# A macaron block of routed feed-forward, attention and routed feed-forward on one core: earlier gathers, sums moved from VectorE to GpSimd, and other orders where the program changes part

## The chip, the core and the metric

The kernel runs on one core of a Trainium2 chip. Its engines are TensorE (PE in the profile; its weight loads PEld), VectorE (DVE), ScalarE (ACT), GpSimd (POOL) and SyncE (SP), which issues most of the DMAs; each works through its own program in order and meets the others at semaphores. The metric is the device time of one execution in microseconds (us), the median of several.

## What is computed

```
x = x + 0.5 * ffn(layernorm(x))       # x: 16 sequences x 512 tokens x 128, float32
x = x + attention(layernorm(x))       # 16 heads of 8, keys = queries = values less their mean
x = x + 0.5 * ffn(layernorm(x))       # the same weights again

ffn(x):  probs = softmax(x @ Wg + bg); w, idx = top_k(probs, 2); w = w / sum(w)
         h = relu(x @ W1[e] + b1[e])  # 8 experts, 256 hidden
         y = h @ W2[e] + b2[e]
         out = sum over e of y[e] * weight of e
attention(x): c = x - mean over the tokens;  softmax(c @ c.T) @ x, head by head
```

## The kernel before

A *dense job* is one sequence that runs through all 8 experts and is multiplied by gates that are zero for the six not chosen. A *routed job* sends each token's row to its two experts: rows are scattered to DRAM (`sorted`), tiles of one expert are run through it in a *tile stream* and stored (`tiles`), and the results are gathered back (`found`), multiplied by their gates and added to x. The program has these parts, in time: dense jobs 0 to 6 of the first feed-forward (0 to 201 us); attention of sequences 0 to 4; a stream of 25 tiles for the nine routed jobs 0 to 8; attention of sequences 5 to 13 (from 449 us), with the routed results gathered and added beside it; a stream of 31 tiles for the twelve routed jobs 9 to 20 of the second feed-forward; attention of sequences 14 and 15 (from 839 us); and dense jobs 7 to 10 (from 899 us), the tail, beside which the routed jobs 9 to 20 are gathered and added. Attention is four head groups (`hg`) of eight units (`k`) per sequence; a unit is two matmuls of scores (L1781), one exponential on ScalarE of 128 x 1024 (L2052), and a mix (L1796).

The order of everything is written out by hand: one program function per engine and part, with tables of numbers that say at which step beside work is put.

In a dense job, step e of the tail has on VectorE: scale of the expert before (`scale`, L1052: (PSUM + bias) x gate into `acc` or one of two `part` buffers), the two halves of the hidden layer two experts ahead (`ffn_halve`, L1020), then for some experts the sum of a `part` into `acc` (`total_up`, L1029), and by the table `ADDED` one half of a routed job's addition to x (`add_half`, L1629). The other sums are on GpSimd (`total_up`, L1277). `ADDS` and `LAST_ADDS` list the experts whose sum VectorE makes, in jobs 7 to 9 and in job 10. A scale of expert e waits until sum e - 2 is made, since `part` has two buffers; scale of expert 1 waits for all sums of the job before. TensorE runs expert m when scale m - 2 has emptied its output bank.

GpSimd's gathers (`collect`, L1736) are eight per routed job. `COLLECTED` says how many stand in each of the 16 steps of sequences 14 and 15, `COLLECTS` how many in each of the 8 steps of jobs 7 to 10, behind that step's sum. `found` has two buffers, so the first gather of job q waits for the addition of job q - 2:

```
reached(pool, sm["c_added"], q - 1)       # q - 1 routed jobs are added
ADDED = {(0, 3): 8, (0, 4): 9, (0, 7): 10, (1, 0): 11, (1, 3): 12, (1, 4): 13, (1, 7): 14, (2, 0): 15, ...
```

An entry of `ADDED` is (dense job less 7, expert): half, where halves 8 and 9 are those of routed job 13, 10 and 11 of job 14, and so on. Routed jobs 9 to 12 are added under the attention. Other work that the steps touch: the gates of a dense job are turned by TensorE (L714), copied by ScalarE (L1193), stored and spread over the partitions by a DMA; the router's logits of a routed job in an attention sequence are a flat matmul (L1347), a copy by VectorE (L1452), a turn by TensorE (`route_turn_logits`, L1353) and a second copy (L1456); norms of attention rows and router rows (`norm_pool`, L652 to L661) are GpSimd's; means for the centring are TensorE's (`attn_means`, L1743). `PAUSES` are the first head groups behind the two tile streams, `RUSH` the sequences 4 and 13 ahead of them, `TILED` is sequence 5.

Of the kernel before, what the change touches and what calls it, by code (L numbers as in the profile page):

```python
# [65 lines left out]
COLLECTED = {14: (1, 1, 1, 1, 1, 1, 1, 2) * 2, 15: (1, 1, 1, 1, 1, 1, 1, 2) * 2}  # L66
COMBINED = {(14, 2): 0, (15, 0): 1, (15, 2): 2, (15, 3): 3}
COLLECTS = [(2, 2, 2, 2, 2, 2, 2, 2)] * 3 + [(2, 2, 2, 2, 2, 2, 0, 0)]
# [3 lines left out]
ADDS = 1, 3, 4, 5  # L72
LAST_ADDS = 1, 3, 4, 5, 6, 7
# [160 lines left out]
def build(nc, x_in, wg_in, bg_in, w1_rows, b1_in, w2_rows, b2_in, const_in, gates_dram, sorted_rows, tile_rows, out):  # L234
    with ExitStack() as ctx:
# [142 lines left out]
        def ring_at(n):  # L378
            k = since_pause(n)
            if leg(n) == 0 or k < RING - 1:  # L380
                return k % RING
            return (0, 1, 5, 2, 3, 4)[(k - RING + 1) % RING]
# [4 lines left out]
        def ring_free(n):  # L387
            return n - (RING - 1 if leg(n) and since_pause(n) == RING - 1 else RING)
# [31 lines left out]
 f_gturned f_gate_rows f_gates_stored f_gates_ahead_even f_gates_ahead_odd f_gates_rest_even f_gates_rest_odd  # L420
# [49 lines left out]
        def _(sp):  # L470
# [101 lines left out]
            for e in range(0, E, AHEAD):  # L572
                sp.wait_ge(sm["w1_shifted"], CHUNKS if e else CHUNKS // 2)
                spread_part(0, e)
# [258 lines left out]
        def ffn_tensor(pe, first, last):  # L833
            if first == 0:
# [5 lines left out]
                ffn_logits(pe, 0)  # L840
                ffn_turn_logits(pe, 0)
# [8 lines left out]
            for n in range(first, last):  # L850
                for e in range(E):
                    m = n * E + e
                    if m == 0:
                        pe.wait_ge(sm["b2_set"], 1)
                        ffn_expert(pe, 0)
                    if m + 2 < last * E:
# [14 lines left out]
                    if m == 0:  # L871
                        ffn_turn_gates(pe, 0)
# [150 lines left out]
        def ffn_vector(dve, first, last):  # L1023
# [10 lines left out]
            def scale(m):  # L1034
# [3 lines left out]
                if e == 0:  # L1038
# [4 lines left out]
                    dve.wait_ge(gates_ahead[u], 16 * uses(n))  # L1043
                    reached(dve, sm["f_back"], before_on_side(n) + 1)
                    into = acc[:, u, :]
                else:
                    reached(dve, sm["f_summed"], n * (E - 1) + (e - 2 if e > 2 else 0))
                    into = part[:, e % 2, :]
                if e == AHEAD:
# [26 lines left out]
            for n in range(first, last):  # L1076
                for e in range(E):
# [41 lines left out]
                    if n == WHOLE - 1:  # L1119
# [6 lines left out]
                        if e == 7:  # L1126
                            route_stats(dve, EARLY)
                    if n < WHOLE:
# [4 lines left out]
            if last < JOBS:  # L1133
                scale(last * E - 1)
            else:
# [59 lines left out]
        def ffn_scalar(act, first, last):  # L1195
# [7 lines left out]
            if first == 0:  # L1203
# [13 lines left out]
                first_half_of_w1(act, 2)  # L1217
                relu(2)
                ffn_copy_gates(act, 0)
# [4 lines left out]
            for n in range(first, last):  # L1224
                for e in range(E):
# [20 lines left out]
                    if e == (AHEAD + 3 if n == 0 else AHEAD + 2 if n == WHOLE else AHEAD + 1) and n < last - 1:  # L1246
                        ffn_copy_gates(act, n + 1)
                    if (n - WHOLE, e) in ADDED:
                        at = ADDED[n - WHOLE, e]
                        scale_half(act, GROUP[1] + at // TOPK, at % TOPK)  # L1250
                    if n < last - 2:
                        if e == 3:
                            ffn_norm_rows_scaled(act, n + 2)
# [124 lines left out]
        def tensor_stream(pe, a, b, at_slot):  # L1378
# [47 lines left out]
            for i in stream(a, b):  # L1426
# [10 lines left out]
                if i == b:  # L1437
                    attn_scores(pe, first + 2)
                if in_stream(i - 1, a, b):
# [371 lines left out]
        def attn_tensor(pe, a, b):  # L1811
            for g in range(a, b):
                s, hg = g // G, g % G
                job, earlier = job_at(s), job_at(s - 1)
                for k in range(UNITS):
                    n = g * UNITS + k
                    if n == 0:
                        attn_mix(pe, 0, 0)
# [514 lines left out]
```

## Time and profile before

| | us |
|---|---|
| three runs | 1018.54, 1017.07, 1015.10 |
| median | 1017.07 |
| the profiled execution | 1015.89 |
| its span, first to last instruction | 1014.1 |
| busy: TensorE, VectorE, ScalarE, GpSimd | 966.3, 795.0, 833.1, 525.9 |
| mean granted TensorE clock (1 is 2.4 GHz) | 0.991 |

All durations below come from the profiled execution, so sums are made against its own time. A busy share is a mean over parts with different limits: it says little until it is taken stage by stage. In a timeline row the first number is the start, the second the length (of several instructions together where there is x2 or more), and the bracket, if any, the idle time of the engine ahead of it and what ended it. In a row of waits stand the instruction that waited, what it waited for, the sum, the number and the longest. A row of busy time by stretch has its from and to, its length, the busy time and instructions of PE, PEld, DVE, ACT and POOL, the granted clock, the share of the DMA engines and GB/s.

### The profile page before, as it was taken

What the parts mean: (1) busy time and instruction counts of PE and PEld (TensorE: products, weight loads), DVE (VectorE), ACT (ScalarE), POOL (GpSimd) and SP (SyncE); (2) the same over time, 40 slices, a digit from 0 to 9 for tenths busy, and PEclk for the clock granted to TensorE, in tenths of its full rate; (3) what the DMA queues carried; (4) which work ended last, traced back from release to release, by engine and by line L of the source; (5) the groups of instructions that cost most, each with busy time, mean ns of one, the idle gap of its engine ahead of it and who ended that gap; (6) DMA issues with size and microseconds to landing.
All of it is one profiled execution on the core that took longest, in us unless ns stands there. A gap on an engine that the chain in (4) does not pass through costs nothing.

```text
span 1014.1 us, 20376 instructions
## 1 busy us (share of the span) xinstructions
PE 966.3 (95%) x6528; PEld 538.1 (53%) x6528; DVE 795.0 (78%) x2271; ACT 833.1 (82%) x1194; POOL 525.9 (52%) x623
## 2 busy tenths in 40 slices
PE   7999999999999999998999999999999999999995
PEld 5687777623223288872332323332588883247774
DVE  5899999967776799875778787778788775469997
ACT  4655554499999988888999999999999989976653
POOL 5546777754434504435676667776200005666775
PEclk7999999999999999999999999999999999999999
DMA  6453232000024224530111111161344431243443
GB/s 187 149 176 133 103 105 105 17 17 20 19 82 124 67 96 161 174 123 24 33 35 35 38 38 38 35 193 51 87 138 145 146 112 60 65 136 112 134 157 124
DMA packets 59821, 96.15 MB, mean 95 GB/s; under 512 B 9179, under 2 KB 30403, under 8 KB 59715
## 3 DMA queue, kind: packets, MB, share of 16 engines
q1 hardware_dynamic: 47568, 71.50, 21.8%
q0 software_dynamic: 10752, 22.04, 7.3%
q10 hardware_dynamic: 1396, 1.31, 0.4%
q8 instruction: 53, 0.87, 0.3%
q14 instruction: 52, 0.43, 0.1%
HBM read 56.36 MB, written 38.45 MB: 94 GB/s over the span
## 4 chain that ended last, share of the span: by engine, by line
PE 54%; ACT 19%; issue 11%; DVE 8%; DMA 3%; POOL 2%; SPq 1%; ACTq 0%; POOLq 0%; DVEq 0%
ACT probs L2052 12%; PE ps L1796 9%; ACT sums L2052 6%; PE ps L1781 5%; PE ps L745 3%; PE ps L1400 3%; PE ps L1401 3%; PE ps L1402 3%; PE ps L761 3%; PE ps L1386 2%; DVE low L1020 2%; PE ps L747 2%; PE ps L1412 2%; PE ps L746 2%; PE ps L1416 2%
## 5 line engine op out<-in xcount | busy, mean ns | idle before, releaser
L2052 ACT ACTIVATE probs<-ps 128x1024 f32<-128x1024 f32 x345 | 353.2, 1156 | 11.0 <-PE ps L1781 10.8
L1736 POOL DMA_INDIRECT found<-tiles,home x168 | 166.9, 993 | 190.2 <-ACT probs L2052 140.3
L1724 POOL DMA_INDIRECT sorted<-xn,slot x168 | 167.5, 997 | 176.3 <-ACT probs L2052 60.7
L1796 PE MATMUL ps<-probs,value 128*32 128x512 f32 x1380 | 243.6, 604 | 3.0 <-ACT probs L2052 1.4
L2052 ACT ACTIVATE sums<-ps 128x1024 f32<-128x1024 f32 x167 | 188.6, 1157 | 2.7 <-PE ps L1781 1.8
L1201 ACT ACTIVATE high<-ps 128x512 fp32r<-128x512 f32 x176 | 101.6, 593 | 71.9 <-PE ps L747 69.8
L1781 PE MATMUL ps<-shared 32*128 32x512 f16 x1024 | 147.7, 384 | 10.4 <-ACT probs L2052 2.8
L1796 PE MATMUL ps<-sums,value 128*32 128x512 f32 x668 | 148.7, 604 | 0.2 <-ACT probs L2052 0.2
L1020 DVE SCALAR_TENSOR_TENSOR low<-ps,high 128x512 fp32r<-128x512 f32 x176 | 112.7, 680 | 8.8 <-ACT high L1201 8.6
L1781 PEld LDWEIGHTS ps<-shared 32*128 32x128 f16 x1024 | 39.2, 91 | 148.1 <-ACT probs L2052 69.1
L1277 POOL TENSOR_TENSOR sums<-sums 128x512 f32<-128x512 f32 x59 | 76.3, 1293 | 60.5 <-DVE sums L1052 48.1
L761 PE MATMUL ps<-high,weights 128*128 128x512 f32 x176 | 72.3, 411 | 7.5 <-DVE sums L1052 7.5
L1642 DVE SCALAR_TENSOR_TENSOR low<-ps,high 128x512 fp32r<-128x512 f32 x112 | 71.9, 683 | 5.4 <-ACT high L1687 2.1
L745 PE MATMUL ps<-xh,weights 128*128 128x512 f32 x176 | 75.9, 431 | 0.0
L1687 ACT ACTIVATE high<-ps 128x512 fp32r<-128x512 f32 x112 | 66.6, 598 | 10.3 <-PE ps L1402 6.2
L1937 DVE COPY shared<-ps 128x1024 f16<-128x1024 f16 x63 | 43.2, 686 | 37.0 <-PE ps L1753 36.9
L746 PE MATMUL ps<-xl,weights 128*128 128x512 f32 x176 | 70.2, 399 | 0.0
L762 PE MATMUL ps<-high,weights 128*128 128x512 f32 x176 | 70.1, 399 | 0.0
L747 PE MATMUL ps<-xh,weights 128*128 128x512 f32 x176 | 70.1, 398 | 0.0
L1675 ACT ACTIVATE chosen<-weights 128x1024 fp32r x56 | 59.2, 1060 | 7.2 <-issue 5.6
L1796 PEld LDWEIGHTS ps<-probs,value 128*32 128x32 f32 x1380 | 35.1, 108 | 42.7 <-issue 34.0
L1753 PEld LDWEIGHTS ps<-K,wide 128*128 128x128 f16 x512 | 29.0, 97 | 51.4 <-issue 50.6
(207 smaller groups left out, 1895.0 us busy)
## 6 DMA issues: line engine op xcount, KB each, us to landing
found<-sorted SPq DMA_DIRECT2D x56, 256.0 KB, 2.7
tiles<-sums SPq DMA_DIRECT2D x56, 256.0 KB
probs<-gates SPq DMA_DIRECT2D x24, 512.0 KB, 5.7
wide<-gates SPq DMA_DIRECT2D x20, 512.0 KB, 6.0
sorted<-zeros SPq DMA_DIRECT2D x16, 512.0 KB
out<-X SPq DMA_DIRECT2D x15, 256.0 KB, 2.4
sorted<-xn,slot POOLq DMA_INDIRECT x168, 2.3
found<-tiles,home POOLq DMA_INDIRECT x168
```

Of the source, the lines that this page charges most:

```text
L745: nc.tensor.matmul(o, weights[:, e, 0, at], xh[:, u, :], start=True, stop=False)
L746: nc.tensor.matmul(o, weights[:, e, 0, at], xl[:, u, :], start=False, stop=False)
L747: nc.tensor.matmul(o, weights[:, e, 1, at], xh[:, u, :], start=False, stop=True).then_inc(sm["f_hidden"], 1)
L761: nc.tensor.matmul(o, weights[:, e, 2, at], high[:, third(m), c, :], start=(c == 0), stop=False)
L1020: nc.vector.scalar_tensor_tensor(low[:, third(m), c, :], ps[:, hidden_bank(m, c), :], 0.0, high[:, third(m), c, :].bitcast(F32), ALU.max, ...
L1201: nc.scalar.activation(high[:, third(m), c, :], ps[:, hidden_bank(m, c), :], ACT.Relu).then_inc(sm["f_high"], 1)
L1277: nc.gpsimd.tensor_tensor(acc[:, side(n), :], acc[:, side(n), :], part[:, e % 2, :], ALU.add).then_inc(sm["f_summed"], 1)
L1724: nc.gpsimd.indirect_dma_start(sorted_rows[group_of(q)], bass.IndirectOffsetOnAxis(ap=slot[:, q % XNS, k, j:j + 1], axis=0), xn[:, rows_sl ...
L1736: nc.gpsimd.indirect_dma_start(found[:, q % 2, k, j, :], None, tile_rows[group_of(q)], bass.IndirectOffsetOnAxis(ap=home[:, q, k, j:j + 1] ...
L1781: ins = nc.tensor.matmul(ps[:, score_banks(n).start + odd, :], kq[at, g % 2, 0, j * P:(j + 1) * P], kq[at, g % 2, 1, :], start=True, stop= ...
L1796: ins = nc.tensor.matmul(ps[q * W:(q + 1) * W, MIX, :], value[:, s % 2, sd, j, m, q, :], ring[ring_at(g * UNITS + 2 * j + q // 2)][:, q % ...
L2052: nc.scalar.activation(ring[ring_at(n)], ps[:, score_banks(n), :], ACT.Exp, scale=SCORE).then_inc(sm["a_probs"], 1)
```

## The change

1. `COLLECTED` grows from 18 to 22 gathers in each of sequences 14 and 15, 44 and not 36 together; the last job's table ends after four.
2. `ADDS` loses expert 4 and `LAST_ADDS` experts 1 and 4: five sums are made by GpSimd.
3. At the start the first two experts' gates are spread apart, their turn on TensorE comes ahead of the third hidden layer and their copy on ScalarE ahead of its relu; nine warm-up matmuls are put between the first logits and their turn.
4. At the start of attention the last dense scale comes ahead of the routing's gate arithmetic, and the scores of two more units ahead of the first mix. Behind each tile stream scores come one unit further ahead, the ring of score buffers has another order there, and the wait for the stream's stores stands at the tenth exponential, not the eighth.
5. In every sequence with a router job the turn of the logits moves from unit 3 to unit 6 of head group 2, its copy on VectorE behind the attention's finish and shift, and the wait for that copy from the back transposes to the turn of the next head group.
6. The means in sequences 4 and 13 move from unit 4 to unit 6. GpSimd's two norms in sequence 5 move ahead of gathers. In the dense jobs ScalarE's norm of rows comes ahead of its half of a routed job.

```diff
@@ -66 +66 @@
-COLLECTED = {14: (1, 1, 1, 1, 1, 1, 1, 2) * 2, 15: (1, 1, 1, 1, 1, 1, 1, 2) * 2}
+COLLECTED = {14: (1, 1, 2, 1, 1, 2, 1, 2) * 2, 15: (1, 1, 2, 1, 1, 2, 1, 2) * 2}
@@ -68 +68 @@
-COLLECTS = [(2, 2, 2, 2, 2, 2, 2, 2)] * 3 + [(2, 2, 2, 2, 2, 2, 0, 0)]
+COLLECTS = [(2, 2, 2, 2, 2, 2, 2, 2)] * 3 + [(2, 2, 0, 0, 0, 0, 0, 0)]
@@ -72,2 +72,2 @@
-ADDS = 1, 3, 4, 5
-LAST_ADDS = 1, 3, 4, 5, 6, 7
+ADDS = 1, 3, 5
+LAST_ADDS = 3, 5, 6, 7
@@ -382 +382 @@
-            return (0, 1, 5, 2, 3, 4)[(k - RING + 1) % RING]
+            return (0, 1, 2, 3, 5, 4)[(k - RING + 1) % RING]
@@ -388 +388 @@
-            return n - (RING - 1 if leg(n) and since_pause(n) == RING - 1 else RING)
+            return n - (RING - 1 if leg(n) and RING - 1 <= since_pause(n) < RING + 3 else RING)
...
@@ -572,2 +572,7 @@
-            for e in range(0, E, AHEAD):
-                sp.wait_ge(sm["w1_shifted"], CHUNKS if e else CHUNKS // 2)
+            sp.wait_ge(sm["w1_shifted"], CHUNKS // 2)
+            sp.wait_ge(sm["f_gates_stored"], 16)
+            for e, signal in ((0, sm["f_first_gate"]), (1, gates_ahead[side(0)])):
+                sp.dma_start(gates_on_all[side(0)][:, e:e + 1, :],
+                             gates_dram[side(0):side(0) + 1, e:e + 1, :].to_broadcast([P, 1, T])).then_inc(signal, 16)
+            sp.wait_ge(sm["w1_shifted"], CHUNKS)
+            for e in range(AHEAD, E, AHEAD):
@@ -840,0 +846 @@
+                keep_warm(pe, 9)
@@ -855,0 +862 @@
+                        ffn_turn_gates(pe, 0)
@@ -871,2 +877,0 @@
-                    if m == 0:
-                        ffn_turn_gates(pe, 0)
@@ -1043 +1048,4 @@
-                    dve.wait_ge(gates_ahead[u], 16 * uses(n))
+                    if n == 0:
+                        dve.wait_ge(sm["f_first_gate"], 16)
+                    else:
+                        dve.wait_ge(gates_ahead[u], 16 * uses(n))
@@ -1048,0 +1057,2 @@
+                if n == 0 and e == 1:
+                    dve.wait_ge(gates_ahead[side(0)], 16)
@@ -1127,0 +1138 @@
+                            scale(last * E - 1)
@@ -1133,3 +1144 @@
-            if last < JOBS:
-                scale(last * E - 1)
-            else:
+            if last == JOBS:
@@ -1218 +1226,0 @@
-                relu(2)
@@ -1219,0 +1228 @@
+                relu(2)
@@ -1247,0 +1257,2 @@
+                    if n < last - 2 and e == 3:
+                        ffn_norm_rows_scaled(act, n + 2)
@@ -1252,2 +1262,0 @@
-                        if e == 3:
-                            ffn_norm_rows_scaled(act, n + 2)
@@ -1438,0 +1448 @@
+                    attn_scores(pe, first + 3)
@@ -1817,0 +1828,2 @@
+                        attn_scores(pe, 2)
+                        attn_scores(pe, 3)
@@ -1819 +1831 @@
-                    if n + 2 < b * UNITS and not (g in PAUSES and k == 0):
+                    if n + 2 < b * UNITS and not (g in (0, *PAUSES) and k < 2):
@@ -1837,0 +1850,2 @@
+                        if hg == 3 and job is not None:
+                            pe.wait_ge(sm["r_lg"], job + 1)
@@ -1850,2 +1863,0 @@
-                    if k == 3 and hg == 2 and job is not None:
-                        route_turn_logits(pe, job)
@@ -1854 +1866 @@
-                            pe.wait_ge(sm["r_lg"], job + 1)
+                            pe.wait_ge(sm["r_flat_copied"], job - EARLY + 1)
@@ -1862 +1874 @@
-                    if k == 4 and hg == 1 and s + 1 < S:
+                    if k == (6 if s in RUSH else 4) and hg == 1 and s + 1 < S:
@@ -1871,0 +1884,3 @@
+                    if k == 6 and hg == 2 and job is not None:
+                        reached(pe, sm["a_normed"], g // SIDES)
+                        route_turn_logits(pe, job)
@@ -1898 +1913 @@
-        def attn_high_rows(dve, s, job):
+        def attn_high_rows(dve, s):
@@ -1904,2 +1918,0 @@
-            if job is not None:
-                route_copy_logits(dve, job)
@@ -2007 +2020 @@
-                    attn_high_rows(dve, s + 1, job)
+                    attn_high_rows(dve, s + 1)
@@ -2014,0 +2028,2 @@
+                if hg == 2 and job is not None:
+                    route_copy_logits(dve, job)
@@ -2047 +2062 @@
-                if n == PAUSES[y] * UNITS + 7:
+                if n == PAUSES[y] * UNITS + 9:
@@ -2102 +2117 @@
-                if i == 2 and more:
+                if i == (0 if s == TILED else 2) and more:
@@ -2104 +2119 @@
-                if i == 4 and job is not None and late(s):
+                if i == (1 if s == TILED else 4) and job is not None and late(s):
```

GpSimd at the beginning of the tail (job 7): a DMA row with `found<-tiles,home` is a gather, one that waits for `c_added` is the first of a routed job, `sums<-sums` is a sum. Before, from the first gathers in job 7:

```order
L1736 DMA found<-tiles,home 128x128 x5
L1736 DMA found<-tiles,home 128x128 [waits c_added,g_home]
L1736 DMA found<-tiles,home 128x128
L1277 TENSOR_TENSOR sums<-sums 128x512 [waits f_summed,f_scaled]
L1736 DMA found<-tiles,home 128x128 x6
L1736 DMA found<-tiles,home 128x128 [waits c_added,g_home]
L1736 DMA found<-tiles,home 128x128
L1277 TENSOR_TENSOR sums<-sums 128x512 [waits f_summed,f_scaled]
L1736 DMA found<-tiles,home 128x128 x2
L1277 TENSOR_TENSOR sums<-sums 128x512 [waits f_summed,f_scaled]
```

With the change:

```order
L1746 DMA found<-tiles,home 128x128 x5
L1746 DMA found<-tiles,home 128x128 [waits c_added,g_home]
L1746 DMA found<-tiles,home 128x128
L1286 TENSOR_TENSOR sums<-sums 128x512 [waits f_summed,f_scaled]
L1746 DMA found<-tiles,home 128x128 x4
L1286 TENSOR_TENSOR sums<-sums 128x512 [waits f_summed,f_scaled]
L1746 DMA found<-tiles,home 128x128 x2
L1746 DMA found<-tiles,home 128x128 [waits c_added,g_home]
L1746 DMA found<-tiles,home 128x128
L1286 TENSOR_TENSOR sums<-sums 128x512 [waits f_summed,f_scaled]
L1746 DMA found<-tiles,home 128x128 x2
L1286 TENSOR_TENSOR sums<-sums 128x512 [waits f_summed,f_scaled]
```

In both a routed job's first gather and one more stand directly ahead of a sum. Before, these first gathers are the 41st and the 49th of the 96, those of routed jobs 14 and 15; with the change they are the 49th and the 57th, those of jobs 15 and 16. The sum behind the four gathers, that of expert 4, is new on GpSimd.

TensorE in head group 2 of an attention sequence with a router job (`shared` are scores, `K,summed` is the turn of the logits, `K,mixed` the back transposes). Before:

```order
L1781 MATMUL ps<-shared 128x512 [waits a_probs]
L1781 MATMUL ps<-shared 128x512
L1353 MATMUL ps<-K,summed 128x128 [waits r_flat_copied]
L1781 MATMUL ps<-shared 128x512 [waits a_probs]
L1781 MATMUL ps<-shared 128x512
L1796 MATMUL ps<-probs,value 32x512 [waits a_probs]
L1796 MATMUL ps<-probs,value 32x512 x3
L1760 MATMUL ps<-K,mixed 128x128 [waits a_copied,a_operands,r_lg]
L1760 MATMUL ps<-K,mixed 128x128 x3
L1781 MATMUL ps<-shared 128x512 [waits a_probs]
```

With the change, from the back transposes on:

```order
L1770 MATMUL ps<-K,mixed 128x128 [waits a_copied,a_operands,r_flat_copied]
L1770 MATMUL ps<-K,mixed 128x128 x3
L1791 MATMUL ps<-shared 128x512 [waits a_probs]
L1791 MATMUL ps<-shared 128x512
L1791 MATMUL ps<-shared 128x512 [waits a_probs,a_operands]
L1791 MATMUL ps<-shared 128x512
L1806 MATMUL ps<-probs,value 32x512 [waits a_probs]
L1806 MATMUL ps<-probs,value 32x512 x3
L1362 MATMUL ps<-K,summed 128x128 [waits r_flat_copied,a_normed]
L1791 MATMUL ps<-shared 128x512 [waits a_probs]
L1791 MATMUL ps<-shared 128x512
L1791 MATMUL ps<-shared 128x512 [waits a_probs]
```

The turn stood between two pairs of scores ahead of the back transposes; it now stands behind them, two pairs of scores and a mix, and the back transposes wait for the flat copy in place of the turned one.

## Rows read from the trace of the kernel before

**Rows 1.** Busy time by stretch, two stretches of the dense tail.
```profile
930.00:960.00 30.00, 27.31 (x127) 20.86 (x126) 28.98 (x58) 20.64 (x54) 23.91 (x25) 1.00 0.39 126
960.00:990.00 30.00, 27.87 (x118) 21.00 (x118) 29.46 (x45) 16.06 (x37) 23.71 (x24) 1.00 0.43 137
```

**Rows 2.** Waits of TensorE, 899 to 1014 us.
```profile
PE ps L761 <- DVE sums L1052: 5.3, 9, 1.0
...
PE ps L681 <- ACT xn L643: 1.2, 1, 1.2
```

**Rows 3.** Timeline, 27 to 31 us, VectorE and TensorE.
```profile
29.10 0.75 DVE L1052 SCALAR_TENSOR_TENSOR sums<-ps,b2T,probs 128x512 f32<-128x512 f32 x1 [2.02 <-issue]
...
29.91 0.52 PE L761 MATMUL ps<-high,weights 128*128 128x512 f32 x1 [1.52 <-DVE sums L1052]
```

**Rows 4.** Busy time by stretch, 30 to 34 us.
```profile
30.00:34.00 4.00, 4.00 (x17) 2.50 (x18) 4.00 (x13) 0.91 (x3) 3.24 (x6) 0.57 0.54 215
```

**Rows 5.** Timeline, 199 to 205 us, VectorE and ScalarE.
```profile
200.87 1.09 DVE L1517 TENSOR_SCALAR den<-second 128x4 f32<-128x4 f32 x1
...
202.36 0.75 DVE L1052 SCALAR_TENSOR_TENSOR sums<-ps,b2T,probs 128x512 f32<-128x512 f32 x1
...
203.91 1.94 ACT L2052 ACTIVATE probs<-ps 128x1024 f32<-128x1024 f32 x2 [1.57 <-PE ps L1781]
```

**Rows 6.** Waits ahead of line L1353, and TensorE's timeline at 250 us.
```profile
  DVE summed L1452: 4.7, 12
...
250.64 0.39 PE L1781 MATMUL ps<-shared 32*128 32x512 f16 x2
...
251.39 0.39 PE L1781 MATMUL ps<-shared 32*128 32x512 f16 x2
```

**Rows 7.** Timeline of ScalarE, 453 to 459 us.
```profile
453.92 1.03 ACT L2052 ACTIVATE probs<-ps 128x1024 f32<-128x1024 f32 x1 [0.42 <-PE ps L1781]
...
458.37 1.02 ACT L2052 ACTIVATE sums<-ps 128x1024 f32<-128x1024 f32 x1 [0.68 <-issue]
```

**Rows 8.** Waits of TensorE, 449 to 475 us.
```profile
PE ps L1333 <- DVE cent L1891: 1.7, 1, 1.7
...
PE ps L1743 <- DVE summed L1884: 0.8, 1, 0.8
```

**Rows 9.** Waits of TensorE, 330 to 345 us, then 700 to 712 us.
```profile
PE ps L1796 <- DVE mixed L1947: 1.0, 1, 1.0
...
PE ps L1743 <- DVE summed L1884: 0.9, 1, 0.9
```

**Rows 10.** Timeline of GpSimd, 931 to 988 us.
```profile
931.80 0.96 POOL L1736 DMA_INDIRECT found<-tiles,home  x1 [0.15 <-POOL sums L1277]
...
934.18 1.30 POOL L1277 TENSOR_TENSOR sums<-sums 128x512 f32<-128x512 f32 x1
...
986.76 1.29 POOL L1277 TENSOR_TENSOR sums<-sums 128x512 f32<-128x512 f32 x1
```

**Rows 11.** Timeline of VectorE, 921 to 991 us.
```profile
921.39 0.68 DVE L1629 TENSOR_TENSOR X<-X,found 128x512 f32<-128x512 f32 x1
921.99 0.74 DVE L1052 SCALAR_TENSOR_TENSOR sums<-ps,b2T,wide 128x512 f32<-128x512 f32 x1
...
927.62 0.74 DVE L1052 SCALAR_TENSOR_TENSOR sums<-ps,b2T,wide 128x512 f32<-128x512 f32 x1
...
936.18 0.66 DVE L1629 TENSOR_TENSOR X<-X,found 128x512 f32<-128x512 f32 x1
...
939.83 0.74 DVE L1052 SCALAR_TENSOR_TENSOR sums<-ps,b2T,probs 128x512 f32<-128x512 f32 x1
...
986.43 2.18 DVE L1629 TENSOR_TENSOR X<-X,found 128x512 f32<-128x512 f32 x1
...
990.39 0.73 DVE L1052 SCALAR_TENSOR_TENSOR sums<-ps,b2T,probs 128x512 f32<-128x512 f32 x1
```

**Rows 12.** Groups of VectorE, 899 to 1014 us: busy us, mean ns, idle before.
```profile
L1629 DVE TENSOR_TENSOR X<-X,found 128x512 f32<-128x512 f32 x16 | 16.9, 1057 | 2.0 <-ACT found L1620 1.9
```

More of the change, by code:

```diff
@@ L419, in build @@
  f_rank f_top f_below f_weight f_picked f_total f_inv f_gate f_again
- f_gturned f_gate_rows f_gates_stored f_gates_ahead_even f_gates_ahead_odd f_gates_rest_even f_gates_rest_odd
+ f_first_gate f_gturned f_gate_rows f_gates_stored f_gates_ahead_even f_gates_ahead_odd f_gates_rest_even f_gates_rest_odd
  f_vare a_vare r_vare f_stats f_hidden f_high f_low f_expert f_scaled f_summed f_back f_added
@@ L1217, in ffn_scalar @@
                 first_half_of_w1(act, 2)
+                ffn_copy_gates(act, 0)
                 relu(2)
-                ffn_copy_gates(act, 0)
                 first_half_of_w2(act, 2)
```

## The prediction

> **What bounds the kernel now.** I read the page first (TensorE is busy for 95% of the span), then busy time by stage, then in each stage that the change touches the waits and the timeline around them, and last, for the dense tail (jobs 7 to 10, from 899 us), each engine's own order of work. In the attention stages ScalarE's exponentials set the pace and TensorE follows them; there the reader is to look for an exponential that starts later than 0.9 us after the one before. In the tail the stage table shows VectorE at 28.98 us of 30 and 29.46 of 30, with TensorE at 27.31 and 27.87 [rows 1]. TensorE's waits there end mostly with a "scale", the VectorE instruction that takes an expert's output from PSUM: nine waits, 5.3 us [rows 2]. So between 930 and 1000 us whatever stops VectorE moves the end, nearly one for one.
>
> The sum is made against the profiled execution, 1015.9 us; the median of the runs shown is 1017.07, 1.2 us above it. A difference of 0.3%, 3 us, is about what a measurement can tell from none.
>
> **The parts ahead of the tail.**
>
> *First gates.* VectorE stands for 2.02 us until scale of expert 0 at 29.10, which waits for the spread gates, and TensorE for 1.52 us behind it, until 29.91 [rows 3]. The 512 KB spread of the first two experts' gates becomes two of 256 KB, and the gates' transposes and copy move ahead of a hidden layer on TensorE and a pair of relu on ScalarE. VectorE's gap is all that can go at once. Behind it the granted clock is 0.57 between 30 and 34 us [rows 4]: half rate for 3.4 of the 4 us, which costs TensorE 1.7 us of work. I take -2.0; from both sides -1.0 (half of the spread's time remains) and -3.7 (the half rate goes too). The nine extra warm-up matmuls stand in front of a transpose that waits for ScalarE anyway; I count nothing for them, and as ends the same 1.7 us of half rate, to either side.
>
> *Start of attention.* ScalarE is idle for 1.57 us ahead of the exponential at 203.91; scale(55) ran only at 202.36, behind the 1.09 us piece of the routing at 200.87 [rows 5]. It is now ahead of that chain, and two more units' scores ahead of the first mix. The unit after next still waits for the back transposes, so of the 1.57 us I take -1.25 (0 to -1.6).
>
> *Turn of the router's logits.* Twelve times the weight load at L1353 waits for VectorE's copy of the flat logits, 4.7 us together [rows 6], and TensorE's next scores stand behind it: they start at 251.39, 0.75 us behind the pair at 250.64, and the exponential that needs them is late by some 0.4. The turn moves three units later, when the copy is long done, and its own copy moves behind VectorE's shift. What is late next is the turn of rows one unit further on, which now also waits for that copy: it comes just in time by my count. -4.7 (-2.5 to -5.2).
>
> *Restarts after the tile streams.* Scores for the fourth unit come with the third: the idle time of 0.42 at 453.92 goes, and its like in the second restart, those of the third units stay. The wait ahead of 458.37, 0.68, which ends with the last stores of the stream, moves two units back [rows 7]. -0.42 x 2 - 0.68 = -1.5 (-0.5 to -2.5).
>
> *Sequence 5.* GpSimd's two norms go ahead of gathers that wait for those stores. TensorE's waits of 1.7 and 0.8 [rows 8] follow from the late norms; the shorter one reaches the exponentials in part only: -2.2 (0 to -2.5).
>
> *Means in sequences 4 and 13.* They move two units later, so that a wait at L1743 in each goes, 0.9 in sequence 13, but the centred rows come that much later on VectorE, where in sequence 4 the mixed copy already holds up TensorE by 1.0 [rows 9]. I count +0.7 for the two (-0.8 to +1.5).
>
> Together -2.0 - 1.25 - 4.7 - 1.5 - 2.2 + 0.7 = **-11.0 us**.
>
> **The tail.** Eight gathers more are done under the attention, where GpSimd has idle time, so in jobs 7 to 9 every gather comes eight places, half a job, earlier. That moves it past something. The gathered rows have two buffers, and the first gather of routed job q waits until job q-2 has been added by VectorE (`c_added`). The additions have not moved. Before, the first gather of job 15 stood at expert 6 of dense job 7 and needed job 13, whose second half is added at expert 4. Now it stands at expert 2 of that job, two steps ahead of what it needs. The same holds six times: at experts 2 and 6 of jobs 7, 8 and 9. GpSimd runs in order, and behind the waiting gather stand the sums that were left to it or are newly given to it: the sum of expert 2, which scale(4) waits for, and the sums of 6 and 7, which the next job's scale(1) waits for. VectorE goes on to the addition (it doesn't need those sums before), and then stands.
>
> Price of one block: two gathers and a sum take from 931.80, where the first gather starts, to 935.48, where the sum of 934.18 ends: 3.7 us [rows 10].
> - At expert 2: the addition ends at 922.07 (921.39 + 0.68) and scale(4) started at 921.99 [rows 11]. It now starts some 3.8 us after the addition: **+3.9**, three times, 11.7.
> - At expert 6: two gathers, a sum, two gathers, a sum, 7.5 us behind the addition at 936.18, which ends at 936.84; scale(1) started at 939.83, 3.0 later [rows 11]. **+4.5**, in jobs 7 and 8, 9.0. In job 9 the addition starts at 986.43, ends at 988.61, and scale(1) is at 990.39: +5.7.
>
> Sum 26.4. Against it stand: VectorE's waits for gathered rows, 1.9 us [rows 12]; the two of the last job's sums that leave VectorE, 2 x 0.68 = 1.4; and the slow additions. Sixteen take 16.9 us [rows 12], 6.0 over 16 x 0.68, since some run beside GpSimd's sums (2.18 at 986.43, with a sum at 986.76 [rows 10, 11]); with GpSimd standing still in front of its waits I give half of that, 3.0. The one sum that leaves VectorE in each of jobs 7 to 9 gains nothing: four gathers now stand between GpSimd's sums of experts 2 and 4, and 2 x 2.4 for them (931.80 to 934.18 for a pair) and 1.3 for the second sum are 6.1, against 5.6 from scale(4) at 921.99 to scale(6) at 927.62. ScalarE's earlier norm saves TensorE a wait of 1.2 [rows 2], which I count at nothing, since VectorE is the later one around it. Tail 26.4 - 6.3 = **+20.1**.
>
> 1015.9 - 11.0 + 20.1 = **1025.0**: slower. Ends: with blocks at two thirds, 17.6 (VectorE catches up between them), all 6.0 of the slow additions gained and gains of 14 ahead of the tail, 1015.9 - 14 + 17.6 - 9.3 = 1010; with no credit at all and gains of 9, 1033.
>
> **Rivals.**
> - *The blocks are hidden and it is faster.* If a block costs less than 11.0 / 6 = 1.8 us on the path, the sign turns. For it: VectorE, freed of waits and of slow additions, and TensorE with two output banks may make up most of a block before the next. Against it: VectorE is at 98% there [rows 1], with little to make it up from. With blocks at nothing 1015.9 - 11.0 - 3.3 (gathered rows and two sums) = 1001.6; between that and 1010 lies this rival. Chance 0.17.
> - *Half and half.* Blocks at 2.5 each are 15, less credits of 6.3, against 11.0: 1013.6, and to 1018 with smaller gains ahead of the tail. Chance 0.12.
> - *The blocks are as reckoned*, 1019 to 1034, likeliest 1025. Chance 0.71, and three things inside it set how far up:
> - *The gains ahead of the tail don't come* (the turn's wait moves one unit on, the norms meet other waits): with half of them, 1030.5. Chance 0.12 of the 0.71.
> - *The sums cost VectorE on GpSimd, too.* One addition beside a sum of GpSimd took 2.18 us, another 0.68 alone [rows 10, 11]. If each of the five moved sums slows one instruction by such 1.5 us, 7.5 come on top: 1032.5. I leave it out of the sum, since the new sums fall beside scales and halves, which read one operand from PSUM. Chance 0.08 of the 0.71. The Trainium skill, "GPSIMD Engine Reference", 1. Specifications, says that GpSimd shares its SBUF interfaces with VectorE and contends with instructions that have two SBUF inputs; the slow addition agrees.
> - *TensorE falls to half rate behind a block.* After waits of TensorE up to 1.52 us the clock was at 0.57 [rows 3, 4]. In the three long blocks TensorE would stand for about 4 us; at 1.7 us of lost work behind each, 5.1 come on top: 1030.1. I leave it out, since VectorE is the later one behind a block. Chance 0.15 of the 0.71. The Trainium skill, "TensorE: Matmul & The Clock Gate", Part 1, says that an idle array drops to 1.2 GHz and that sustained work brings back 2.4; the first 34 us of this trace agree.
>
> The range 1010 to 1034 leaves out the hidden blocks below, 0.17, and some 0.03 above. Faster 0.17, same 0.12, slower 0.71.
>
> **What would show it.** Right: in jobs 7 to 9 GpSimd idle for several us in front of a gather, ended by VectorE's addition; VectorE idle for about 3.5 us ahead of scale(4) and 4.5 ahead of scale(1), ended by GpSimd's sum; tail of some 135 us instead of 115; no wait at the turned logits; the dense tail beginning about 11 us earlier. Wrong: gathers of the tail that never wait for an addition, or a tail no longer than before.

## The result and the profile after

| | before | after |
|---|---|---|
| median of the runs, us | 1017.27 (4) | 1035.91 (4) |
| ratio after / before | | 1.0186, 95% interval 1.0163 to 1.0209 |
| span of the profiled execution, us | 1014.1 | 1035.1 |
| first exponential of attention, start | 199.39 | 197.80 |
| scale of expert 3 in dense job 7, start | 919.54 | 911.30 |
| last scale, start | 1006.36 | 1028.24 |
| from the one scale to the other ("tail" below) | 86.8 | 116.9 |

Slower, as forecast, and by more: 1035.9 lies above the range, whose top was 1034. The medians differ by 18.6 us, the two profiled executions by 21.0. In these the part ahead of the tail is 8.2 us shorter and the tail 30.1 us longer, where 11.0 and 20.1 were forecast, and 0.8 us is saved behind the last scale.

Busy time by stretch of the changed kernel, for [rows 1]:

```profile
930.00:960.00 30.00, 20.81 (x87) 15.29 (x86) 17.80 (x37) 11.09 (x28) 17.75 (x20) 0.89 0.32 98
960.00:990.00 30.00, 23.64 (x90) 18.04 (x90) 20.60 (x37) 13.08 (x33) 15.29 (x16) 0.89 0.30 96
```

Where VectorE was busy for 28.98 and 29.46 of 30 us, it is now busy for 17.8 and 20.6, and TensorE for 20.8 and 23.6. In these stretches no engine is the limit any more; all of them stand for a part of the time. The waits of VectorE and then of TensorE in the changed kernel, 899 to 1036 us (its lines: L1062 scale, L1286 GpSimd's sum, L1639 addition, L732 the back transposes of the job before, L766 the first matmul of an expert), for [rows 2]:

```profile
DVE sums L1062 <- POOL sums L1286: 30.6, 10, 6.1
DVE X L1639 <- ACT found L1630: 5.1, 3, 3.1
...
PE ps L732 <- POOL sums L1286: 15.3, 3, 5.6
PE ps L766 <- DVE sums L1062: 10.3, 7, 3.2
```

Scales wait 30.6 us in ten places for sums of GpSimd; before there was no such row. That GpSimd itself waits is in its timeline, for [rows 10]:

```profile
914.58 0.94 POOL L1746 DMA_INDIRECT found<-tiles,home  x1 [5.95 <-DVE X L1639]
915.83 0.94 POOL L1746 DMA_INDIRECT found<-tiles,home  x1 [0.30 <-issue]
916.80 1.27 POOL L1286 TENSOR_TENSOR sums<-sums 128x512 f32<-128x512 f32 x1
...
932.57 0.94 POOL L1746 DMA_INDIRECT found<-tiles,home  x1 [5.94 <-DVE X L1639]
...
938.44 1.27 POOL L1286 TENSOR_TENSOR sums<-sums 128x512 f32<-128x512 f32 x1
```

A gather stands for 5.95 us until an addition, the sum comes after it, and the same again at 932.57. There are six such gathers, the others at 952.95, 969.91, 988.86 and 1004.92: two each in jobs 7, 8 and 9. VectorE's side, for [rows 11]:

```profile
913.15 0.68 DVE L1639 TENSOR_TENSOR X<-X,found 128x512 f32<-128x512 f32 x1
...
918.10 0.75 DVE L1062 SCALAR_TENSOR_TENSOR sums<-ps,b2T,wide 128x512 f32<-128x512 f32 x1 [4.27 <-POOL sums L1286]
...
924.29 0.75 DVE L1062 SCALAR_TENSOR_TENSOR sums<-ps,b2T,wide 128x512 f32<-128x512 f32 x1 [1.07 <-POOL sums L1286]
...
931.16 0.65 DVE L1639 TENSOR_TENSOR X<-X,found 128x512 f32<-128x512 f32 x1
...
939.74 0.75 DVE L1062 SCALAR_TENSOR_TENSOR sums<-ps,b2T,probs 128x512 f32<-128x512 f32 x1 [3.61 <-POOL sums L1286]
...
949.06 0.69 DVE L1639 TENSOR_TENSOR X<-X,found 128x512 f32<-128x512 f32 x1 [3.07 <-ACT found L1630]
```

The addition ends at 913.83, the scale behind it starts at 918.10; the other ends at 931.81, and scale of expert 1 starts at 939.74. The last row is new in its size: after the long block VectorE waits 3.07 us more, for ScalarE (L1630, its half of a routed job), where before the addition at this place waited 0.22. What TensorE does around it, in its timeline and by stretches of 4 us:

```profile
939.76 1.11 PE L732 MATMUL ps<-K,sums 128*128 128x128 f32 x4 [5.55 <-POOL sums L1286]
```

```profile
937.00:941.00 4.00, 1.24 (x5) 1.24 (x6) 1.26 (x2) 0.00 (x0) 3.33 (x4) 0.73 0.14 35
941.00:945.00 4.00, 4.00 (x11) 3.03 (x11) 2.93 (x6) 1.20 (x2) 3.55 (x6) 0.50 0.13 33
945.00:949.00 4.00, 4.00 (x20) 3.08 (x19) 0.99 (x2) 2.95 (x10) 0.97 (x2) 0.92 0.17 41
```

TensorE stands for 5.55 us at the back transposes of the job before, which need all sums, and then runs at a granted clock of 0.50, the lower of its two levels (1.2 GHz): 11 matmuls in 4 us, where 20 fit in the next 4. ScalarE, on which VectorE waits, waits itself for TensorE there (L719 turns the gates):

```profile
946.05 0.27 ACT L1202 ACTIVATE shared<-ps 32x128 f32<-32x128 f32 x1 [1.98 <-PE ps L719]
```

The first exponential stood between 0.6 us later and 3.5 us earlier than before in the profiled executions of the changed kernel and of eleven below with the same code up to there, and 1.4 us earlier in one whose code up to there is that of before (e2). So the experiments are read by the ratio of their times and, for the tail, by the length from scale of expert 3 in job 7 to the last scale in each trace. That length can be trusted: where the tail's code is the same (e4 and e8, e7 and e10) it agrees within 0.1 us. The part ahead of it can't be read from one trace: in the six executions with the changed kernel's code up to there (the changed kernel, e3, e5, e6, e9, e12) it was 6.9 to 12.3 us shorter than in the one of the kernel before, 9.7 in the mean.

### The profile page after: what moved, and what is told of

Read it like the earlier page. It is cut to its first block, busy times and chain, and to the rows that moved or that the text cites. A ratio compares the mean times of both kernels' runs of the same rounds, so it can differ in the third digit from the quotient of the medians.

```text
span 1035.1 us, 20426 instructions
## 1 busy us (share of the span) xinstructions
PE 973.2 (94%) x6546; PEld 545.9 (53%) x6546; DVE 788.3 (76%) x2266; ACT 831.9 (80%) x1194; POOL 531.3 (51%) x628
## 4 chain that ended last, share of the span: by engine, by line
PE 39%; ACT 27%; issue 17%; DVE 9%; POOL 4%; DMA 2%; ACTq 0%; POOLq 0%; DVEq 0%; SPq 0%
ACT probs L2067 17%; ACT sums L2067 8%; DVE low L1025 3%; PE ps L1806 3%; PE ps L1409 3%; PE ps L1411 2%; PE ps L1410 2%; PE ps L1395 2%; PE ps L1425 2%; PE ps L1421 2%; PE ps L1420 2%; PE ps L1432 2%; PE ps L766 2%; PE ps L750 2%; PE ps L767 2%
## 5 line engine op out<-in xcount | busy, mean ns | idle before, releaser
L2067 ACT ACTIVATE probs<-ps 128x1024 f32<-128x1024 f32 x345 | 343.0, 1216 | 5.9 <-PE ps L1791 5.8
L2067 ACT ACTIVATE sums<-ps 128x1024 f32<-128x1024 f32 x167 | 179.0, 1220 | 2.9 <-PE ps L1791 2.6
L1791 PE MATMUL ps<-shared 32*128 32x512 f16 x1024 | 142.1, 385 | 8.9 <-ACT probs L2067 2.4
L1286 POOL TENSOR_TENSOR sums<-sums 128x512 f32<-128x512 f32 x64 | 82.8, 1293 | 51.0 <-DVE sums L1062 45.5
L766 PE MATMUL ps<-high,weights 128*128 128x512 f32 x176 | 74.1, 421 | 11.7 <-DVE sums L1062 11.6
L767 PE MATMUL ps<-high,weights 128*128 128x512 f32 x176 | 71.9, 409 | 0.0
L771 PE MATMUL ps<-low,weights 128*128 128x512 f32 x176 | 57.2, 407 | 0.0
```

The costliest lines, as they stand in the source:

```text
L766: nc.tensor.matmul(o, weights[:, e, 2, at], high[:, third(m), c, :], start=(c == 0), stop=False)
L767: nc.tensor.matmul(o, weights[:, e, 3, at], high[:, third(m), c, :], start=False, stop=False)
L1286: nc.gpsimd.tensor_tensor(acc[:, side(n), :], acc[:, side(n), :], part[:, e % 2, :], ALU.add).then_inc(sm["f_summed"], 1)
L1791: ins = nc.tensor.matmul(ps[:, score_banks(n).start + odd, :], kq[at, g % 2, 0, j * P:(j + 1) * P], kq[at, g % 2, 1, :], start=True, stop= ...
L2067: nc.scalar.activation(ring[ring_at(n)], ps[:, score_banks(n), :], ACT.Exp, scale=SCORE).then_inc(sm["a_probs"], 1)
```

## The experiments

Each ratio is to the kernel before, measured beside it, with its 95% interval; the profiles are one execution each.

| | median us | ratio | tail us |
|---|---|---|---|
| before | | 1 | 86.8 |
| after | 1035.9 | 1.0186 (1.0163 to 1.0209) | 116.9 |
| e1: after with 36 gathers | 1012.3 | 0.9973 (0.9952 to 0.9995) | 89.6 |
| e2: before with 44 gathers | 1038.7 | 1.0230 (1.0204 to 1.0257) | 113.0 |
| e3: after, sums 2 and 4 on VectorE | 1020.1 | 1.0063 (1.0040 to 1.0086) | 101.4 |
| e4: after, gathers behind additions | 1009.3 | 0.9950 (0.9930 to 0.9971) | 89.2 |
| e5: after, 85 warm matmuls | 1068.8 | 1.0526 (1.0508 to 1.0544) | 152.2 |
| e6: after, back transposes later | 1033.2 | 1.0166 (1.0146 to 1.0186) | 113.6 |
| e7: e4, five sums as before | 1004.0 | 0.9885 (0.9869 to 0.9902) | 83.5 |
| e8: e4, means and norm | 1005.5 | 0.9900 (0.9883 to 0.9917) | 89.3 |
| e9: after, 20 warm matmuls | 1029.9 | 1.0153 (1.0117 to 1.0189) | 111.6 |
| e10: e4 with e7 and e8 | 1000.0 | 0.9847 (0.9818 to 0.9876) | 83.5 |
| e11: e10 with 36 gathers | 1004.7 | 0.9892 (0.9865 to 0.9920) | 87.1 |
| e12: after, five sums as before | 1031.9 | 1.0179 (1.0147 to 1.0212) | 113.2 |

**e1, the gathers' tables as before.**

```diff
-COLLECTED = {14: (1, 1, 2, 1, 1, 2, 1, 2) * 2, 15: (1, 1, 2, 1, 1, 2, 1, 2) * 2}
-COLLECTS = [(2, 2, 2, 2, 2, 2, 2, 2)] * 3 + [(2, 2, 0, 0, 0, 0, 0, 0)]
+COLLECTED = {14: (1, 1, 1, 1, 1, 1, 1, 2) * 2, 15: (1, 1, 1, 1, 1, 1, 1, 2) * 2}
+COLLECTS = [(2, 2, 2, 2, 2, 2, 2, 2)] * 3 + [(2, 2, 2, 2, 2, 2, 0, 0)]
```

> The changed kernel with the two tables of gathers as before (36 under the last two sequences), all else as changed. Theory 1, the tail's loss is the gathers that wait for an addition ahead of GpSimd's sums: no gather in the tail waits for an addition, the tail from the first dense scale to the end is 105 to 108 us as before or a little less, and the time is 1005 to 1009 us. Rival, the loss comes from the five sums that GpSimd took over or from the other orders in the dense jobs: the time stays above 1020.

1012.3 us. The two tables alone carry the loss: 27.3 of the 30.1 us of the tail are gone with them. But the time misses the range of theory 1 upwards, and the tail is 2.8 us longer than before where it should have been no longer. VectorE's waits in this tail:

```profile
DVE X L1639 <- ACT found L1630: 7.1, 5, 2.4
DVE sums L1062 <- POOL sums L1286: 1.9, 1, 1.9
```

Additions waited 1.9 us for gathered rows before [rows 12]; with five sums more on GpSimd, in front of gathers, they wait 7.1. So the moved sums seem to cost something without any block, which e7 tests.

**e2, the kernel before with the new tables**: e1's diff the other way round, on the kernel before.

> The kernel before with the two tables of gathers alone as changed (44). Theory 1: the sums of experts 2, 6 and 7 were GpSimd's before too, so all six blocks appear, 4.3 us at expert 2 and 7.9 at expert 6 behind the addition, and the time is 1040 to 1047 us. Rival, the moved sums are needed for the loss: 1017 to 1025.

1038.7 us. In its tail scales wait for GpSimd's sums six times:

```profile
DVE sums L1052 <- POOL sums L1277: 26.1, 6, 6.1
```

Just below the range of theory 1, far above the rival's: the block needs neither the moved sums nor any of the new orders.

**e3, the sums of experts 2 and 4 on VectorE.**

```diff
-ADDS = 1, 3, 5
+ADDS = 1, 2, 3, 4, 5
```

> The changed kernel, but VectorE makes the sums of experts 2 and 4 in jobs 7 to 9, so that nothing VectorE needs in the middle of a job stands behind a waiting gather; the three blocks at expert 6 stay. Theory 1: the waits of 4.3 us ahead of scale of expert 4 vanish, the three waits of TensorE behind them (2.6 to 3.2 us) too, six sums of 0.68 come on VectorE: 9 to 13 us faster than the changed kernel, 1023 to 1027. Rival, TensorE and VectorE are held by the tail's other work and only shift their waits: within 3 us of the changed kernel.

1020.1 us, a little better than expected; tail 15.5 us shorter. Its waits of scales for GpSimd are down to

```profile
DVE sums L1062 <- POOL sums L1286: 14.0, 4, 6.1
```

from 30.6 in ten places. A gather still waits at expert 2 (6.57 us in front of 913.68), and costs nothing there: what counts is not the gather's wait but the sum behind it.

**e4, gathers one step behind the additions that they wait for.**

```diff
-COLLECTS = [(2, 2, 2, 2, 2, 2, 2, 2)] * 3 + [(2, 2, 0, 0, 0, 0, 0, 0)]
+COLLECTS = [(2, 2, 0, 0, 0, 2, 2, 2)] + [(2, 2, 2, 2, 2, 2, 2, 2)] * 2 + [(2, 2, 2, 2, 2, 0, 0, 0)]
```

> The changed kernel with 44 gathers under the last two sequences, but none at experts 2 to 4 of job 7, so that every first gather of a routed job stands one step behind the addition that it waits for. Theory 1: no gather waits for more than 1 us for an addition, and the time is 1003 to 1008 us, at most some 2 us better than with 36, since two buffers allow no more lead. Rival, earlier gathers as such collide with other work of the tail: slower than with 36 by 3 us or more.

No gather of its tail waits for an addition, and it is faster than before: ratio 0.9950. Three scales still wait for GpSimd's sums:

```profile
DVE sums L1062 <- POOL sums L1286: 5.7, 3, 2.7
```

1009.3 us is 1 us above the range, and the tail no shorter than in e1, 89.2.

**e5 and e9, TensorE kept at work in front of the long blocks' end.**

```diff
                     if e == 2 and n > first:
+                        if n > WHOLE:
+                            for _ in range(85):
+                                nc.tensor.matmul(ps[:, MISC, 0:D], ones[:, :], zeros[:, :], start=True, stop=True)
                         ffn_back(pe, n - 1)
```

> The changed kernel with 85 matmuls of zeros on TensorE ahead of the back transposes of the job before, in dense jobs 8 to 10, where TensorE stands for 4.6 to 5.6 us and the granted clock falls to half behind it. Theory 2, part of the loss beyond the waits themselves is TensorE's half rate behind the long blocks (0.50 from 941 to 945 us): the clock stays at 1.0 there and the time falls by 3 to 6 us. Rival, VectorE is the later one behind a block, as the prediction had it: within 1.5 us of the changed kernel.

1068.8 us, which decides nothing: each call is two passes, 85 of them ran from 930.5 to 949.6 us, 19 us in front of transposes that were ready some 13 us sooner (GpSimd's last sum of the block ends at 936.2). e9 is the same with 20.

> The changed kernel with 20 and not 85 matmuls of zeros ahead of the back transposes in dense jobs 8 to 10: the 85 took 19 us each time (170 passes from 930.5 to 949.6), so 20 take about 4.5 us, inside waits of 4.6 to 5.6. Theory 2, TensorE's half rate behind the long blocks costs: the clock stays at 1.0 from the block on and the time falls by 3 to 6 us. Rival, VectorE is the later one behind a block and the half rate costs nothing: within 1.5 us of the changed kernel.

1029.9 us and a tail 5.4 us shorter than the changed kernel's. TensorE's zeros in the first long wait, and stretches of 4 us in e9 (the sums end about 4 us earlier in it):

```profile
930.02 4.63 PE L887 MATMUL ps<-zeros,ones 128*128 128x128 f32 x40
```


```profile
933.00:937.00 4.00, 2.90 (x23) 2.58 (x23) 1.27 (x3) 0.00 (x0) 3.33 (x4) 1.00 0.13 35
937.00:941.00 4.00, 4.00 (x20) 3.16 (x18) 3.73 (x7) 2.24 (x5) 3.56 (x6) 1.00 0.14 37
```

The clock stays at 1.00, 20 matmuls run where 11 did, and scale of expert 3 follows scale of expert 2 after 6.1 us, not 8.1 (3.8, not 6.6, in job 9). Besides these two only scale of expert 4 in job 10 comes earlier against the scale before it, by 0.6 us; no other distance between two scales differs by more than 0.05. The two intervals of the ratios overlap; the traces tell them apart. So half rate costs what e9 gives back, some 5 us.

**e6, the back transposes one expert later.**

```diff
-                    if e == 2 and n > first:
+                    if e == (3 if n > WHOLE else 2) and n > first:
                         ffn_back(pe, n - 1)
```

> The changed kernel with the back transposes of the job before one expert later on TensorE in dense jobs 8 to 10. Theory 3, TensorE itself stands behind GpSimd's sums at these transposes, with a hidden layer and an expert behind them that it could run under the wait, and the pipeline has to be filled again after it: 5 to 9 us faster than the changed kernel. Rival, the blocks cost what VectorE waits and no more: within 2 us.

1033.2 us, tail 3.3 us shorter: between the two. The intervals of the ratios overlap here, too, so this is read from the traces. TensorE now runs a hidden layer under the wait and stands at the expert behind it, 4.98 us until 941.93, so the clock falls as before (0.63 from 941 to 945 us). Part of the refilling is gone, the half rate is not.

**e7, e4 with the five sums back on VectorE.**

```diff
-ADDS = 1, 3, 5
-LAST_ADDS = 3, 5, 6, 7
+ADDS = 1, 3, 4, 5
+LAST_ADDS = 1, 3, 4, 5, 6, 7
```

> The variant without blocks (44 gathers, none at experts 2 to 4 of job 7), with the five sums back on VectorE. Theory 4, the moved sums cost in the last job, where VectorE waited 1.6 and 2.7 us for GpSimd's sums: 2 to 4 us faster than that variant. Rival, they free VectorE as intended: 2 to 4 us slower.

Ratio 0.9885 against 0.9950, tail 83.5 against 89.2: 5.7 us, more than expected. One scale waits for GpSimd now, and additions wait 1.5 us for gathered rows:

```profile
DVE X L1639 <- ACT found L1630: 1.5, 3, 0.8
...
DVE sums L1062 <- POOL sums L1286: 0.6, 1, 0.6
```

Moving the sums was a loss by itself, without any block.

**e8, e4 with the means of sequence 4 at unit 4 and the norm of sequence 14 first.**

```diff
-                    if k == (6 if s in RUSH else 4) and hg == 1 and s + 1 < S:
+                    if k == (6 if s == RUSH[1] else 4) and hg == 1 and s + 1 < S:
...
-                if i == (0 if s == TILED else 2) and more:
+                if i == (0 if s in (TILED, S - 2) else 2) and more:
```

> The variant without blocks, with the means of sequence 4 at unit 4 as before (those of sequence 13 stay at 6), and GpSimd's attention norm of sequence 14 ahead of its first gathers, as in sequence 5. Theory 5, the means cost 2.9 us in sequence 4 and the norm behind waiting gathers 1.3 in sequence 14: 3.5 to 4.3 us faster than that variant, no wait of TensorE for the mixed copy over 1.2 us and none for the sum of the rows in sequence 14. Rival, the time is only moved to the next wait of VectorE: within 1.5 us.

Ratio 0.9900 against 0.9950, about 5 us by the times. TensorE's waits around the mixed copy of sequence 4 are first those of the changed kernel and then those of e8:

```profile
PE ps L1806 <- DVE mixed L1960: 2.5, 1, 2.5
```

```profile
PE ps L1806 <- DVE mixed L1960: 1.0, 1, 1.0
PE ps L1753 <- DVE summed L1899: 0.8, 1, 0.8
```

The wait of 0.8 that the change removed is back, and the one of 2.5 that it made is gone. Across sequence 4 (from its first exponential to that of sequence 5) e4 fell back 2.8 us against the kernel before, e8 only 0.2; in sequence 14, which is 0.7 us shorter than in e4, e8 has no wait for the sum of the rows. Nor have e10 and e11, which have its edit; without it seven executions of nine waited there, 0.9 to 1.9 us, and e3 and e5 did not. What the times show beyond 2.6 and 0.7 us stays open. This execution lost 1.8 us in the second tile stream, in which no code differs, so its trace shows less ahead of the tail than the sum.

**e10 and e11, the parts together, with 44 gathers and with 36.**

> 44 gathers with none at experts 2 to 4 of job 7, the five sums back on VectorE, the means of sequence 4 at unit 4, the norm of sequence 14 first. If the parts add (e7 won 5.7 us in the tail by the trace, e8 2.4 and more ahead of it): 1000 to 1003 us. If they share a wait: 1003 to 1006.

> The same with the gathers' tables as before (36). If the eight early gathers are worth something by themselves, through VectorE's waits for gathered rows in the tail: 2 to 4 us slower than with 44. If the two buffers take away any lead: within 1.5 us.

1000.0 us, ratio 0.9847: 1.5% faster than before, and the fastest kernel here. With 36 gathers it is 1004.7, and the tail 3.6 us longer. VectorE's waits for ScalarE's gathered rows and for GpSimd's sums in the two tails (e10, then e11):

```profile
DVE X L1639 <- ACT found L1630: 1.0, 2, 0.8
...
DVE sums L1062 <- POOL sums L1286: 0.6, 1, 0.6
```

```profile
DVE X L1639 <- ACT found L1630: 4.8, 2, 3.6
...
DVE sums L1062 <- POOL sums L1286: 0.6, 1, 0.6
```

So the lead of eight gathers is worth about 4 us, when it is used behind the additions and not ahead of them. One gather of e10 still stands for 4.65 us, until an addition just ahead of 910.71, and no scale waits for what is behind it. With the old tables of gathers e11 also parts two things that e1 had together: its tail is as long as before (87.1 against 86.8), so the other orders in the dense jobs cost nothing there on balance, and 2.5 us shorter than e1's, which is the price of the five sums with those tables.

**e12, the changed kernel with e7's edit of the five sums.**

> The changed kernel, blocks and all, with the five sums back on VectorE. If the moved sums cost in the blocked tail what they cost in the unblocked one (GpSimd's sum of expert 4 stands behind four gathers and is waited for by scale of expert 6): the tail 4 to 6 us shorter than the changed kernel's, 1030 to 1032. If they are hidden in the blocks' waits: within 2 us.

1031.9 us, and the tail 3.8 us shorter; the ratio, 1.0179, can't be told from 1.0186. By the trace the moved sums cost in the blocked tail, too, a little less than expected. Scales wait for GpSimd in the six blocks alone, and not 30.6 us in ten places:

```profile
DVE sums L1062 <- POOL sums L1286: 26.1, 6, 6.1
```

## Why the prediction was wrong, and what of it was right

The mechanism stands: six gathers at experts 2 and 6 of jobs 7 to 9 wait for additions that haven't moved, and GpSimd's sums behind them hold up scales of experts 4 and 1. e1 and e2 show that the tables of gathers alone make it, e3 that it goes through the sums, e4 that with the same 44 gathers and without it the kernel is faster than before. The size was missed: the tail is 10.0 us longer than forecast. Measured from scale to scale against the kernel before, that is 2.6 of blocks, 5.2 behind the long blocks and 2.2 ahead of scale of expert 6; all else is -6.3, and -6.3 had been credited. The largest of the three is one sentence on TensorE's half rate: "I leave it out, since VectorE is the later one behind a block." Without the half rate the time would have stood inside the range (e9: 1029.9, or 1032.8 by its ratio). For the moved sums, whose cost the sum also left out, this can't be said: without them it is 1031.9, but 1035.5 by the ratio (e12).

**The tail, +20.1 forecast, +30.1 measured.**
- *Blocks, 26.4.* Scale of expert 4 lost 4.3 us three times, scale of expert 1 4.9, 4.9 and 6.2: 29.0. The terms were 3.9, 4.5 and 5.7. What was short is the first step: from an addition's end (913.83) to the gather's start (914.58) 0.75 us pass, in all six, where 0.1 was taken. Two gathers and the sum took 3.5 us and not 3.7.
- *Half rate, 0 in the sum.* The rival was worked out at 5.1 us and left out, "since VectorE is the later one behind a block". It isn't: VectorE made the scales of two experts, at 939.74 and 941.60, and then waited for ScalarE, at last 3.07 us until 949.06, and ScalarE for TensorE. The distance from scale of expert 2 to that of expert 3 grew by 2.9 us in job 8 and 2.2 in job 9 (in job 10 it shrank by 0.5, with 0.6 more behind it), and e9 gave back 5.4 us, at these places alone. This is the step that failed. In it the prediction also missed that the back transposes stand in TensorE's own queue, waiting for the same sums, so that it can't work ahead; e6 gave back 3.3. Both act between the scales of experts 2 and 3, so the two overlap, and their sum was not tried.
- *The five sums, -1.4.* They were said to gain 1.4 in the last job and nothing in the others. In the blocked tail they cost 3.8 us (e12), in the unblocked one 5.7 (e7): scales of expert 6 wait 1.07 us (row at 924.29; 1.06 and 1.67 in jobs 8 and 9) for a sum behind four gathers, and in e12 these waits are gone, 2.1 us of the 3.8. The prediction had reckoned 6.1 against 5.6 us for that pair, 6.2 was measured (918.10 to 924.29), and it then dropped the difference.
- *Credits.* Nearly all of the slow additions went: sixteen take 11.4 us, not 16.9 [rows 12], 5.5 against a credit of 3.0. The waits for gathered rows did not go, 5.1 us and not 1.9, since ScalarE was late behind the long blocks. That the credits come out right together is luck: each of the three was wrong.

**Ahead of the tail, -11.0 forecast, -8.2 in the changed kernel's trace.** Over the six executions of this code it is -9.7 in the mean, from -6.9 to -12.3, so the sum was nearly right. The places, in the one trace:
- *First gates*, -2.0: -1.6 at the first exponential, with the spread told above, in which the kernel before alone has 1.4; the middle one of the twelve is -1.7, so some 1 us is shown, not 2. Scale of expert 0 starts at 27.82 without a wait, and the half rate of [rows 4] is gone:

```profile
30.00:34.00 4.00, 4.00 (x25) 2.96 (x24) 3.50 (x13) 2.98 (x9) 3.08 (x6) 1.00 0.27 109
```

- *Start of attention*, -1.25: -1.2 by the fifth exponential, -1.5 by the tenth. Right.
- *Turn of the logits*, -4.7: about -4.5 over twelve sequences, between 0.2 and 0.6 each. Right; the next turn of rows doesn't wait. The turn of the logits has a wait again, for VectorE, of 0.3 us at most, eight times, 2.0 in all.
- *Restarts and sequence 5*, -1.5 and -2.2: -3.5 from the first exponential of sequence 5 to the second of its third head group, and -0.6 at the second restart. What was not seen is sequence 14: there the norm still stands behind gathers that wait for the stores, and TensorE waited 1.3 us for the rows' sum (0 to 1.9 in the executions without e8's edit). e8 moved the norm and has no such wait.
- *Means*, +0.7: +2.9 in sequence 4 and -0.8 at the means of sequence 13 (-0.5 by its end), so +2.1. The sign of each was right, the size in sequence 4 was not: the wait for the mixed copy, 1.0 [rows 9], became 2.5, and another wait, of ScalarE, 1.4, came two units later. e8 shows that it was the means. That second wait is missing in e5 and e9, which have the same code there and lost 1.3 us in sequence 4 and not 2.9.

Over the rivals: the hidden blocks and the half-price blocks are out by the blocks' 29.0 us and by e2, the contention of GpSimd's sums with VectorE's additions was there before and went with the change. What forecast a higher time, half rate behind the long blocks, was real.

## What to carry to other kernels

- Work that is started earlier in an in-order queue can reach a wait that it never met, for a buffer that another engine gives back at an unchanged place; count for each moved item what it needs and when that is ready, and price not its wait but what stands behind it in that queue. Here the new tables of gathers lost 24 us on the kernel before; with all gathers behind the fourth of job 7 held back by three steps, and the sums left on VectorE, they won 4 (e10 against e11).
- An engine that stands for several microseconds can have a second bill. Here TensorE ran empty under VectorE's waits, came back at half rate and had to be filled again: 3 to 5 us on top of 29 (e6, e9).
- Taking an operation off the busiest engine pays only if the engine that gets it answers in time: five sums of 0.68 us on VectorE cost 2.5 to 6 us on GpSimd (e1 against e11, e12, e7), where they stood among its gathers.

## What the runs showed that was not expected

- GpSimd's first gather started 0.75 us after the end of the addition that released it, the same in all six blocks; the sums behind gathers started 0.02 to 0.03 us after them.
- With 4.6 us of matmuls of zeros in front of a wait of 1.1 us the granted clock stayed at 1.00 (2.4 GHz; e9), where after 5.55 us without work it was 0.50 (1.2 GHz) for 4 us. In the changed kernel's start the clock was 1.00 from 30 to 34 us, where it had been 0.57 [rows 4].
- In equal code the first exponential moved by 4 us between executions, and a tile stream could lose 1.8 us: gains of 1 to 2 us are read from waits in the trace, not from one execution's span.
